# A state-space mixer's loop over batches, written out as straight code on every engine

## The chip, the cores and the metric

The kernel runs on one core of a Trainium2 chip (trn2). Its five engines (PE for matrix products, DVE for vector work, ACT for activations, POOL, and SP, which here only issues transfers) each run an instruction stream of their own and meet through semaphores. The metric is the device time of one execution in microseconds, the median over several.

## The reference

The input has 8 batches of 1024 tokens with 256 features. Three blocks follow each other: a feed-forward block on 4-bit quantised values, a selective-scan mixer, and the feed-forward block once more. The change touches only the mixer:

```python
x = x + 0.5 * ffn(layernorm(x))
x = x + mixer(layernorm(x))          # the part that the change touches
x = x + 0.5 * ffn(layernorm(x))

# mixer, per batch: 512 channels, 16 states each, 1024 steps in time
xz = norm(h) @ in_proj_w;  x, z = split(xz)
x = silu(causal_conv4(x))
delta = softplus((x @ x_proj_w)[:, :64] @ dt_proj_w + dt_proj_b)
h_t = exp(delta_t * A) * h_(t-1) + delta_t * B_t * x_t       # per channel and state
y_t = sum over states of h_t * C_t  +  D * x_t
out = (y * silu(z)) @ out_proj_w
```

The 512 x 16 sequences in time of a batch are worked on as 64 tiles of 128 partitions and 1024 steps, a tile being 8 channels with 16 states.

## The kernel before

`mixer` cuts its work into rounds, one for a batch. A round has 64 **slots**, and a slot does one of the 64 scan tiles: PE repeats the rows of delta times x onto the 128 partitions (`replicate`, L1226, into `mix_ps_du`), DVE multiplies them by B (L1102), ACT takes the exponential for the decay (L1037, into `mix_decay`, whose rows SP spreads by a transfer, L876, six slots ahead), DVE runs the scan (L1086, into `mix_scan`), POOL multiplies by C (L929), and PE sums over the states (`sum_quad`, L1208 and L1212, into `mix_ps_y`). So DVE has a product and a scan in every slot.

Between them lies the rest of the layer, spread over the slots by a table, `JOBS`: small matrix products of kinds T, P, C, X, B, D, Z and O (transpose, in-projection, convolution, x-projection, B and C, delta, gate, out-projection), most of them for the batch of the next round; O is for the batch before. For O, DVE adds the residual (L1116); at slot 4 of every 16 it gates the finished chunk (L1111); BN_STATS and BN_AGGR (L1127, L1135) belong to the norm of the next batch. Each engine has its own function `program(r, R, full)`, which emits one round: `r` decides at build time which parts exist and which half of each double buffer is used, and `R` is the round's number, from which every count that a semaphore is waited for is worked out, and every address in DRAM.

`rounds` calls `program` for r from -1 to 8, ten rounds. Round -1 only prepares batch 0, round 8 only finishes batch 7. Rounds -1, 0, 7 and 8 are straight code. Rounds 1 to 6 are a hardware loop on each engine (`Fori`): three iterations with two rounds in each, in which `R` is a register expression, `it * 2 + 1` or `it * 2 + 2`. So at the end of round 2 and of round 4 each engine branches back, and at the end of round 6 it falls through. There every count and address comes out of register instructions, such as

```python
n = R * 64 + (slot + 1)
dve.wait_ge(exp_done, n)
dve.wait_ge(dbu_done, n)
if slot >= 8 or r > 0:
    dve.wait_ge(y_made, R * 16 + (slot - 8) // 4 + 1)
```

at L1082 to L1085. The engines go around the loop on their own: there is no barrier at its end. The feed-forward blocks have loops of their own (`span`, L32).

## Time and profile before

| | |
|---|---|
| median of 3 runs | 3338.32 us (3337.11 to 3343.49) |
| the profiled execution, its own time | 3331.19 us |
| its span, first to last instruction | 3329.3 us |
| first scan of round 0 to last of round 7 | 750.17 to 2704.05 us |
| mean granted TensorE clock | 0.884 |

The views used below are: a table of stretches of time, with the busy time of each engine; the timeline of one engine, with the idle time in front of an instruction and what ended it in square brackets (nothing stands there where the idle time is under about 0.1 us); and the list of waits of one engine. "issue" as the reason means that nothing that the profile records (no semaphore, no transfer) ended the wait. Register and branch instructions have no rows of their own in these views; they show only as idle time of the engine. Round r begins here with the scan of its slot 0 on DVE.

### The profile page before, as it was taken

The numbers are of one execution on the slowest core, as the hardware profiler recorded it, in microseconds if no ns is written. First come the engines' busy times: TensorE is split into PE (matmuls) and PEld (weight loads), VectorE is DVE, ScalarE is ACT, GpSimd is POOL, SyncE is SP. The second block draws the span as 40 slices with busy tenths as digits, with TensorE's granted clock in tenths as the row PEclk, the third lists the DMA queues.
The fourth block names the chain that finished last, engine by engine and source line by source line (L and its number), as shares of the span: only waits on it lengthen the run. The fifth ranks groups of instructions, "written<-read, shape, count | busy, mean of one in ns | idle before, by whom it ended". The sixth has DMA issues, their size and how long they took to land. (4 is left out here: it accounts for less than half of the span.)

```text
span 3329.3 us, 33530 instructions
## 1 busy us (share of the span) xinstructions
PE 2725.0 (82%) x10221; PEld 1387.1 (42%) x10221; DVE 2664.6 (80%) x2530; ACT 1682.9 (51%) x2331; POOL 2171.1 (65%) x1219
## 2 busy tenths in 40 slices
PE   3999999767877878868878868878867658999999
PEld 1556556542424414414414414414312124656565
DVE  6777777309998998988998998998999956777774
ACT  3444444246664665764665764665664513444442
POOL 4555554218877877877877877877877734555552
PEclk9999999887978978978978978978977669999999
DMA  3011100018686775776776775775876820100100
GB/s 101 19 32 32 32 26 22 26 29 200 161 191 155 171 180 155 180 172 155 169 182 155 183 169 155 176 176 155 187 176 160 204 85 24 32 26 32 32 26 19
DMA packets 164631, 379.73 MB, mean 114 GB/s; under 512 B 21990, under 2 KB 81446, under 8 KB 164198
## 3 DMA queue, kind: packets, MB, share of 16 engines
q1 hardware_dynamic: 146678, 358.67, 44.0%
q10 hardware_dynamic: 17776, 18.94, 2.0%
q8 instruction: 81, 1.33, 0.2%
q14 instruction: 96, 0.79, 0.1%
HBM read 308.26 MB, written 44.11 MB: 106 GB/s over the span
## 5 line engine op out<-in xcount | busy, mean ns | idle before, releaser
L929 POOL TENSOR_TENSOR mix_scan<-mix_scan,mix_bc 128x1024 f32<-128x1024 f32 x512 | 1205.8, 2357 | 436.7 <-DVE mix_scan L1086 436.2
L1086 DVE TENSOR_TENSOR_SCAN mix_scan<-mix_decay,mix_ps_du 128x1024 f32<-128x1024 f32 x512 | 1169.5, 2284 | 70.3 <-ACT mix_decay L1037 27.0
L1226 PE MATMUL mix_ps_du<-mix_stack,mix_sel 96*128 96x512 bf16 x1024 | 371.2, 451 | 430.3 <-DVE mix_scan L1086 397.8
L1102 DVE TENSOR_TENSOR mix_ps_du<-mix_ps_du,mix_bc 128x1024 f32<-128x1024 f32 x512 | 618.3, 1208 | 97.8 <-PE mix_ps_du L1226 85.1
L649 PE MATMUL ffn_ps_gate_up<-ffn_w_gate_up,ffn_xT 128*128 128x512 f32 (+1 forms) x1536 | 662.4, 568 | 14.6 <-DVE ffn_h L456 13.0
L1037 ACT ACTIVATE mix_decay<-mix_decay,mix_a_neg 128x1024 f32<-128x1024 f32 x512 | 571.5, 1141 | 146.0 <-DMA mix_decay<-delta_rows 140.6
L679 PE MATMUL ffn_ps_down<-ffn_w_down,ffn_hT 128*128 128x256 f32 (+1 forms) x1536 | 388.5, 395 | 11.4 <-ACT ffn_hT L584 11.4
L1226 PEld LDWEIGHTS mix_ps_du<-mix_stack,mix_sel 96*128 96x128 bf16 x1024 | 77.1, 103 | 765.9 <-DVE mix_scan L1086 646.1
L649 PEld LDWEIGHTS ffn_ps_gate_up<-ffn_w_gate_up,ffn_xT 128*128 128x128 f32 x1536 | 273.5, 191 | 281.5 <-issue 231.2
L456 DVE TENSOR_TENSOR ffn_h<-ffn_silu_gate,ffn_ps_gate_up 128x704 f32<-128x704 f32 x128 | 113.6, 887 | 302.7 <-ACT ffn_silu_gate L589 302.7
L1208 PE MATMUL mix_ps_y<-mix_scan,mix_red 128*32 128x512 f32 x2048 | 344.6, 755 | 4.8 <-POOL mix_scan L929 4.8
L570 POOL TENSOR_TENSOR ffn_h_scaled<-ffn_h,ffn_h_recip 128x1408 f32<-128x1408 f32 x64 | 184.8, 2888 | 225.1 <-ACT ffn_h_recip L629 225.1
L679 PEld LDWEIGHTS ffn_ps_down<-ffn_w_down,ffn_hT 128*128 128x128 f32 (+1 forms) x1536 | 277.1, 192 | 107.7 <-issue 57.1
L1167 PE MATMUL mix_ps_job<-mix_xin,mix_conv_diag 128*128 128x256 f32 x1024 | 271.5, 414 | 19.9 <-ACT mix_xin L982 19.8
L583 ACT ACTIVATE ffn_hT<-ffn_ps_turned 128x640 f32<-128x640 f32 x128 | 90.1, 704 | 325.8 <-PE ffn_ps_turned L661 325.8
L1167 PEld LDWEIGHTS mix_ps_job<-mix_xin,mix_conv_diag 128*128 128x128 f32 x1024 | 206.6, 207 | 106.3 <-issue 46.9
L564 POOL TENSOR_TENSOR ffn_hq<-ffn_h_scaled,ffn_h_scale 128x1408 f32<-128x1408 f32 x64 | 165.8, 2590 | 78.1 <-DVE ffn_h_scaled L509 73.9
L550 POOL TENSOR_TENSOR ffn_mv<-ffn_mv,ffn_eps 128x2 f32<-128x2 f32 x64 | 33.1, 517 | 253.5 <-DVE ffn_mv L491 249.0
L988 ACT ACTIVATE mix_u<-mix_ps_job,mix_conv_b 128x256 f32<-128x256 f32 x128 | 60.6, 474 | 206.2 <-PE mix_ps_job L1167 205.6
L1188 PE MATMUL mix_ps_job<-mix_hnT,mix_w_in 128*128 128x512 f32 x256 | 147.4, 705 | 6.5 <-ACT mix_hnT L967 6.4
L1160 PE MATMUL mix_ps_job<-mix_hnT,mix_w_in 128*128 128x256 f32 x512 | 131.1, 402 | 4.2 <-ACT mix_hnT L967 3.5
L1194 PE MATMUL mix_ps_job<-mix_w_out,mix_u 128*128 128x256 f32 x512 | 131.9, 417 | 1.4 <-DVE mix_u L1111 1.4
(131 smaller groups left out, 3515.0 us busy)
## 6 DMA issues: line engine op xcount, KB each, us to landing
mix_decay<-delta_rows SPq DMA_DIRECT2D x512, 512.0 KB, 7.5
mix_stack<-mix_parts SPq DMA_DIRECT2D x384, 64.0 KB, 2.0
delta_rows<-mix_delta SPq DMA_DIRECT2D x32, 512.0 KB, 3.1
ffn_x<-_attn_hidden_states_dram SPq DMA_DIRECT2D x32, 256.0 KB, 2.9
after_ffn<-ffn_y SPq DMA_DIRECT2D x32, 256.0 KB, 3.0
mix_x_tokens<-after_ffn SPq DMA_DIRECT2D x32, 256.0 KB, 5.5
mix_x_residual<-after_ffn ACTq DMA_DIRECT2D x32, 256.0 KB, 5.6
after_mixer<-mix_x_residual ACTq DMA_DIRECT2D x32, 256.0 KB, 5.1
```

The lines of the kernel that those rows point to most:

```text
L564: G.tensor_tensor(blocks(hq[:, l2, :]), blocks(hn[:, l2, :]), spread(hs[:, (j - 1) % 4, :]), ALU.mult).then_inc(sig.hq_done, 1)
L570: G.tensor_tensor(blocks(hn[:, j % 2, :]), blocks(h[:, j % 2, :]), spread(hr[:, :]), ALU.mult).then_inc(sig.hn_done, 1)
L649: ins = M(psG[:, lo:hi], xT[:, j % 2, (t * KX + k) * P:(t * KX + k + 1) * P], wgu[:, k, lo:hi], start=(k == 0), stop=(k == KX - 1))
L679: ins = M(psD[:, t, 0:D], hT[0:c, t, k * P:(k + 1) * P], wd[0:c, k, :], start=(k == 0), stop=(k == KH - 1))
L929: G.tensor_tensor(wt, wt, bc[:, r % 2, 1, :], ALU.mult).then_inc(hc_done, 1)
L1037: A.activation(da[:, at % SPREADS, :], da[:, at % SPREADS, :], ACT.Exp, scale=const.aneg[:, qi:qi + 1]).then_inc(exp_done, 1)
L1086: V.tensor_tensor_scan(w[:, slot % RING, :], da[:, slot % SPREADS, :], ps_du[:, slot % 2, :], 0.0, ALU.mult, ALU.add).then_inc(scan_done, 1)
L1102: V.tensor_tensor(ps_du[:, slot % 2, :], ps_du[:, slot % 2, :], bc[:, r % 2, 0, :], ALU.mult)\
L1167: ins = M(job[:, 0:QT], const.conv_diag[:, c, t, :], xin[:, c, t:t + QT], start=(t == 0), stop=(t == TAPS - 1))
L1188: ins = M(job, const.w_in[:, k, DI + c * P:DI + (c + 1) * P], hnT[:, par, k, h * 512:(h + 1) * 512], start=(k == 0), stop=(k == KD - 1))
L1208: ins = M(y[32 * q:32 * q + 32, :], const.red[:, i, :, :].rearrange("p a b -> p (a b)"), w[:, (4 * m + q) % RING, h * 512:(h + 1) * 512], ...
L1226: ins = M(ps_du[:, slot % 2, h * 512:(h + 1) * 512], const.sel[0:SEL, i, :], stack[:, c % 2, q, h * 512:(h + 1) * 512], start=True, stop=True)
```

## The change

`rounds` calls `program(r, r, False)` for all ten rounds, so that no loop is left in the mixer. With a plain number for `R`, every count is a constant in the wait, and every DRAM address a constant in the transfer. `full` was true in the loop only; for r from 1 to 6 the conditions in which it stands (`full or r + 1 < B`, `full or r >= 1`, `core`) come out the same, and so does the list of jobs. What is computed, and in which order, stays as it was.

```diff
-            pairs = (B - 2) // 2
-            for r in range(-1, 1):
-                program(r, r, False)
-            if pairs > 0:
-                with eng.Fori(0, pairs) as it:
-                    for k in range(2):
-                        program(1 + k, it * 2 + (1 + k), True)
-            for r in range(1 + 2 * pairs, B + 1):
+            for r in range(-1, B + 1):
                 program(r, r, False)
```

Seven lines go, so a line number L of the mixer before is L - 7 after, from L811 on.

The order of DVE's instructions at the end of the loop's body, before the change; the last product and scan are those of slot 63 of an even round (the scan is named SCALAR_TENSOR_TENSOR in these lists):

```order
L1086 SCALAR_TENSOR_TENSOR mix_scan<-mix_decay,mix_ps_du 128x1024 [waits mix_y_made,mix_dbu_done,mix_exp_done]
L1095 REGISTER_ALU
L1102 TENSOR_TENSOR mix_ps_du<-mix_ps_du,mix_bc 128x1024 [waits mix_rep_du]
L1086 SCALAR_TENSOR_TENSOR mix_scan<-mix_decay,mix_ps_du 128x1024 [waits mix_y_made,mix_dbu_done,mix_exp_done]
L811 REGISTER_ALU
L811 COMPARE_AND_BRANCH
```

The branch leads back to the top of the body, the first instructions of an odd round on DVE (ISA stands for a fused register instruction):

```order
L811 ISA
L1097 ISA [waits mix_rep_du]
L1102 TENSOR_TENSOR mix_ps_du<-mix_ps_du,mix_bc 128x1024 [waits mix_taken_B]
L1085 ISA [waits mix_dbu_done,mix_exp_done]
L1086 SCALAR_TENSOR_TENSOR mix_scan<-mix_decay,mix_ps_du 128x1024 [waits mix_y_made]
L1095 REGISTER_ALU
```

After the change, the same place on DVE, from the product of slot 62 of round 2 to the scan of slot 0 of round 3:

```order
L1095 TENSOR_TENSOR mix_ps_du<-mix_ps_du,mix_bc 128x1024 [waits mix_rep_du]
L1079 SCALAR_TENSOR_TENSOR mix_scan<-mix_decay,mix_ps_du 128x1024 [waits mix_y_made,mix_dbu_done,mix_exp_done]
L1095 TENSOR_TENSOR mix_ps_du<-mix_ps_du,mix_bc 128x1024 [waits mix_rep_du]
L1079 SCALAR_TENSOR_TENSOR mix_scan<-mix_decay,mix_ps_du 128x1024 [waits mix_y_made,mix_dbu_done,mix_exp_done]
L1095 TENSOR_TENSOR mix_ps_du<-mix_ps_du,mix_bc 128x1024 [waits mix_taken_B,mix_rep_du]
L1079 SCALAR_TENSOR_TENSOR mix_scan<-mix_decay,mix_ps_du 128x1024 [waits mix_y_made,mix_dbu_done,mix_exp_done]
```

The counter, the branch and the five register instructions are gone, and the product of slot 0 carries both of its waits itself.

Within a round on DVE, before the change: from behind the scan of slot 59 to the product of slot 61, in an even round. In front of the scan of slot 60, the first of a group of four, for which the count of `y_made` goes up by one, stands a register instruction which carries two of its three waits:

```order
L1095 REGISTER_ALU
L1102 TENSOR_TENSOR mix_ps_du<-mix_ps_du,mix_bc 128x1024 [waits mix_rep_du]
L1085 REGISTER_ALU [waits mix_dbu_done,mix_exp_done]
L1086 SCALAR_TENSOR_TENSOR mix_scan<-mix_decay,mix_ps_du 128x1024 [waits mix_y_made]
L1095 REGISTER_ALU
L1102 TENSOR_TENSOR mix_ps_du<-mix_ps_du,mix_bc 128x1024 [waits mix_rep_du]
```

After the change these slots read as the rows of the seam shown above do: product, scan, product, scan, with nothing between them, and the scan has its three waits again.

On PE the end of the loop's body, before (slots 62 and 63 of an even round), and under it the top of the body:

```order
L1226 MATMUL mix_ps_du<-mix_stack,mix_sel 128x512 [waits mix_scan_done]
L1226 MATMUL mix_ps_du<-mix_stack,mix_sel 128x512
L1208 MATMUL mix_ps_y<-mix_scan,mix_red 32x512 [waits mix_hc_done]
L1208 MATMUL mix_ps_y<-mix_scan,mix_red 32x512 x7
L811 REGISTER_ALU
L811 COMPARE_AND_BRANCH
```

```order
L811 ISA
L1224 ISA [waits mix_stacked_du0]
L1226 MATMUL mix_ps_du<-mix_stack,mix_sel 128x512 [waits mix_scan_done]
L1226 MATMUL mix_ps_du<-mix_stack,mix_sel 128x512
L1226 MATMUL mix_ps_du<-mix_stack,mix_sel 128x512 [waits mix_scan_done]
L1226 MATMUL mix_ps_du<-mix_stack,mix_sel 128x512
L1248 ISA
```

After the change, PE's same place between rounds 2 and 3:

```order
L1219 MATMUL mix_ps_du<-mix_stack,mix_sel 128x512 [waits mix_scan_done]
L1219 MATMUL mix_ps_du<-mix_stack,mix_sel 128x512
L1201 MATMUL mix_ps_y<-mix_scan,mix_red 32x512 [waits mix_hc_done]
L1201 MATMUL mix_ps_y<-mix_scan,mix_red 32x512 x7
L1219 MATMUL mix_ps_du<-mix_stack,mix_sel 128x512 [waits mix_scan_done,mix_stacked_du0]
L1219 MATMUL mix_ps_du<-mix_stack,mix_sel 128x512
L1219 MATMUL mix_ps_du<-mix_stack,mix_sel 128x512 [waits mix_scan_done]
```

Here too the matrix products stand in the same order, and the first two `replicate` of the next round follow the last sum directly.

## Rows read from the trace of the kernel before

**Rows 1.** The page, its costliest groups (line, counts, busy us, mean ns, idle before)

```profile
L1086 DVE TENSOR_TENSOR_SCAN mix_scan<-mix_decay,mix_ps_du 128x1024 f32<-128x1024 f32 x512 | 1169.5, 2284 | 70.3 <-ACT mix_decay L1037 27.0
...
L1102 DVE TENSOR_TENSOR mix_ps_du<-mix_ps_du,mix_bc 128x1024 f32<-128x1024 f32 x512 | 618.3, 1208 | 97.8 <-PE mix_ps_du L1226 85.1
```

**Rows 2.** Stretches of time, one for each of rounds 0 to 7

```profile
core 0: us, PE busy (x) PEld busy (x) DVE busy (x) ACT busy (x) POOL busy (x), PEclk, DMA share, GB/s
750.17:984.17 234.00, 177.36 (x676) 73.89 (x675) 224.25 (x148) 152.44 (x180) 189.69 (x100) 0.83 0.77 181
984.17:1231.58 247.41, 196.78 (x760) 89.68 (x759) 227.81 (x152) 151.07 (x179) 191.00 (x101) 0.85 0.71 171
1231.58:1483.22 251.64, 196.98 (x764) 89.01 (x763) 227.89 (x152) 152.22 (x181) 192.22 (x101) 0.85 0.72 173
1483.22:1729.86 246.64, 191.85 (x758) 87.36 (x758) 227.60 (x153) 150.14 (x178) 189.88 (x100) 0.86 0.69 165
1729.86:1980.95 251.09, 196.46 (x763) 89.05 (x763) 227.93 (x152) 151.68 (x180) 192.13 (x101) 0.85 0.72 174
1980.95:2228.32 247.37, 195.73 (x759) 89.33 (x758) 227.82 (x153) 150.91 (x179) 189.88 (x100) 0.84 0.68 165
2228.32:2473.03 244.71, 193.64 (x761) 87.95 (x761) 227.76 (x152) 151.28 (x179) 190.94 (x101) 0.86 0.71 171
2473.03:2704.05 231.02, 155.24 (x504) 41.61 (x502) 221.23 (x135) 108.22 (x107) 174.05 (x76) 0.68 0.67 162
```

**Rows 3.** Timeline of DVE, end of round 2 (start, us, instruction, idle before)

```profile
1472.82 2.29 DVE L1086 TENSOR_TENSOR_SCAN mix_scan<-mix_decay,mix_ps_du 128x1024 f32<-128x1024 f32 x1
1481.79 1.23 DVE L1102 TENSOR_TENSOR mix_ps_du<-mix_ps_du,mix_bc 128x1024 f32<-128x1024 f32 x1 [6.68 <-issue]
1483.22 2.29 DVE L1086 TENSOR_TENSOR_SCAN mix_scan<-mix_decay,mix_ps_du 128x1024 f32<-128x1024 f32 x1 [0.20 <-DVE mix_ps_du L1102]
```

**Rows 4.** Timeline of PE and of POOL, the same place

```profile
1478.22 1.89 PE L1226 MATMUL mix_ps_du<-mix_stack,mix_sel 96*128 96x512 bf16 x4 [5.47 <-issue]
...
1485.59 2.36 POOL L929 TENSOR_TENSOR mix_scan<-mix_scan,mix_bc 128x1024 f32<-128x1024 f32 x1 [8.06 <-DVE mix_scan L1086]
```

**Rows 5.** Timeline of DVE, end of round 4

```profile
1971.16 2.29 DVE L1086 TENSOR_TENSOR_SCAN mix_scan<-mix_decay,mix_ps_du 128x1024 f32<-128x1024 f32 x1
1979.52 1.23 DVE L1102 TENSOR_TENSOR mix_ps_du<-mix_ps_du,mix_bc 128x1024 f32<-128x1024 f32 x1 [6.07 <-issue]
```

**Rows 6.** Timeline of DVE, end of round 6, where the loop is left

```profile
2469.53 2.29 DVE L1086 TENSOR_TENSOR_SCAN mix_scan<-mix_decay,mix_ps_du 128x1024 f32<-128x1024 f32 x1
2471.74 1.21 DVE L1102 TENSOR_TENSOR mix_ps_du<-mix_ps_du,mix_bc 128x1024 f32<-128x1024 f32 x1
```

**Rows 7.** Timeline of DVE, slots 27 to 29 of round 1

```profile
1097.68 2.29 DVE L1086 TENSOR_TENSOR_SCAN mix_scan<-mix_decay,mix_ps_du 128x1024 f32<-128x1024 f32 x1
...
1101.29 2.29 DVE L1086 TENSOR_TENSOR_SCAN mix_scan<-mix_decay,mix_ps_du 128x1024 f32<-128x1024 f32 x1 [0.19 <-DVE mix_ps_du L1102]
...
1104.79 2.29 DVE L1086 TENSOR_TENSOR_SCAN mix_scan<-mix_decay,mix_ps_du 128x1024 f32<-128x1024 f32 x1
```

**Rows 8.** Waits of DVE in rounds 1 to 6 (total us, times, longest)

```profile
DVE mix_ps_du L1102 <- issue: 12.8, 2, 6.7
DVE mix_scan L1086 <- DVE mix_ps_du L1102: 12.4, 59, 0.6
```

**Rows 9.** Waits of DVE, straight code: round 0, then round 7

```profile
DVE mix_scan L1086 <- DVE mix_ps_du L1102: 0.2, 1, 0.2
...
DVE mix_scan L1086 <- issue: 0.9, 2, 0.4
```

**Rows 10.** Timeline of PE at slot 17, in round 1 and in round 2

```profile
1056.67 3.42 PE L1167 MATMUL mix_ps_job<-mix_xin,mix_conv_diag 128*128 128x256 f32 x8
...
1303.79 2.00 PE L1167 MATMUL mix_ps_job<-mix_xin,mix_conv_diag 128*128 128x256 f32 x8
```

**Rows 11.** Stretches of time around these two, with the granted clock

```profile
1054.00:1063.00 9.00, 8.13 (x27) 4.26 (x28) 8.84 (x8) 3.56 (x5) 7.21 (x8) 0.81 0.74 170
1300.00:1309.00 9.00, 7.37 (x31) 3.49 (x30) 8.91 (x7) 4.53 (x7) 6.72 (x8) 1.00 0.76 191
```

**Rows 12.** DMA queues in rounds 1 to 6 (packets, MB, share)

```profile
q8 instruction: 44, 0.72, 0.2%
q14 instruction: 61, 0.50, 0.1%
```

## The prediction

> **What bounds the kernel now.** I first read the groups of the page, for DVE's two instructions of a slot: a product of 1208 ns and a scan of 2284 ns [rows 1], together 3.49 us. Two scans that follow without an idle mark start 3.50 us apart, 1104.79 - 1101.29 [rows 7]. So in a plain slot DVE works without a gap and sets the pace; 64 such slots are 224 us. Next I cut the time into rounds. In every one DVE is busy for 221 to 228 us out of 231 to 252, while PE reaches at most 197, POOL 192 and ACT 152 [rows 2]. The whole mixer is thus DVE's chain, and what the change is worth is read from the idle time of DVE, and from nothing else.
>
> The same table has an experiment in it: rounds 0 and 7 are straight code already, rounds 1 to 6 are the loop. Rounds 2 and 4, which end in a taken branch, last 251.64 and 251.09 us; round 6, the same code but left at its end, 244.71 [rows 2]. The odd rounds 1, 3 and 5 last 247.41, 246.64 and 247.37. Round 0 has no O jobs and round 7 nothing of a next batch, so their 234.00 and 231.02 are not to be set against the loop's as a whole; single waits can be.
>
> **Term 1: the two branches back.** What the reader is to see at the end of round 2: the scan of slot 63 starts at 1472.82, the product after it only at 1481.79, with 6.68 us idle that no semaphore and no transfer ended, and the next scan at 1483.22 [rows 3]. PE stood idle too, 5.47 us, also for "issue", and POOL 8.06 us [rows 4]. Each engine comes to its own branch at its own time; PE, which runs ahead, has its gap first, and DVE's own gap is what the chain has to bear. From scan to scan it is 1483.22 - 1472.82 = 10.40 us. Where the same code goes on without a branch back, the product follows the scan after 2471.74 - 2469.53 = 2.21 us [rows 6], and the next scan 3.50 us after the first, as in round 6 (2473.03 is where its stretch ends [rows 2]). The seam thus costs 10.40 - 3.50 = 6.90 us, of which 0.10 is the register work of term 2; I count 6.80. At the end of round 4 it is 1980.95 - 1971.16 = 9.79 us [rows 2, 5], so 9.79 - 3.61 = 6.18. Together **13.0 us**.
>
> Is that pause given back in the round behind it, because the other engines catch up? Round 3 and round 5 follow a pause, round 1 follows straight code: 246.64 and 247.37 against 247.41 [rows 2]. So 0.8 and 0.0 us are given back, and 12.2 is the lower bound of this term, 13.0 the upper. I take 13.0: rounds 5 and 1 agree to 0.04, and the 0.8 has another likely cause, below.
>
> What the Trainium skill has on it: "Runtime: NRT & Kernel Launch", section "Instruction fetch mechanics", says that fetching ahead is sequential only and that a taken branch to a target which isn't held any more makes the engine wait for its code. The 6.68 us of "issue" are what this looks like here.
>
> **Term 2: register instructions.** The loop works its counts out in registers. Most of it is done under a running scan or product and costs nothing: plain slots of the loop last 3.50 us too [rows 7]. But where the count for `y_made` goes up, once in four slots, the register instruction in front of the scan (slot 28 in the rows) also carries the wait for the product, so it can't run before that has ended: 0.19 us idle, and 1101.29 - 1097.68 = 3.61 us in place of 3.50. The loop's six rounds have 59 such waits, 12.4 us in total [rows 8]; round 0, straight, has one [rows 9]. The regular ones are some nine to ten a round and cost 0.10 to 0.11 each beyond a plain slot. The few that are longer, up to 0.6, are ended by something else too. With 54 x 0.10 I take **5.4 us**; the upper bound is 59 x 0.11 = 6.5, the lower one 0, if the second wait, now in an instruction of its own, takes the same time. I take the value near the upper end, since round 0 has exactly that form and just one mark.
>
> **What costs nothing.** The register work of PE, ACT, POOL and SP, and SP's addresses: these engines have 50 to 100 us of slack in a round [rows 2]. If that cover were gone, it would show as DVE waiting for PE or ACT, as it does around the O jobs in the first 16 slots, and a shorter PE or ACT would help there; I count no gain. The number of matrix products, activations and transfers is unchanged. Entry into the loop costs one more 0.1. What was late at the seam was the code alone; the next thing DVE would wait for there is PE's `replicate`, which in straight code comes 2 slots ahead and is ready.
>
> **The sum.** 13.0 + 5.4 = 18.4 us. The profiled execution's own 3331.19 becomes 3312.8, its span of 3329.3 becomes 3310.9. The median of the runs shown lies 7.1 above the profiled one, 3338.32; with the same difference the median after is **3319.9 us**, 0.55% less.
>
> **The term that can't be placed: TensorE's clock.** The odd rounds are longer than the even ones without their seams: the odd mean is 247.14; the even are 251.64 - 6.80 = 244.84, 251.09 - 6.18 = 244.91 and 244.71, mean 244.82. The 2.3 us come from PE. Eight matrix products of the convolution jobs of slot 17 take 3.42 us in round 1 and 2.00 in round 2 [rows 10], because the granted clock was 0.81 of full speed in that stretch, part of it at 1.2 GHz, against 1.00, all at 2.4 GHz [rows 11]; ACT then waits for PE, and DVE for ACT. Nothing in the code differs there. It depends on how the clock's falls meet the slots, and that repeats because an iteration of the loop always lasts the same. Without the seams every round is shifted against them. If all six rounds look like the even ones, 3 x 2.3 = 7 us more are gained; if all look like the odd ones, 7 are lost. I take the middle, no change, and give the range the 7 on both sides: gains of 11.4 to 25.4, or 3313 to 3327. About 3 us of spread between runs (3337.11 to 3343.49) widens it to 3310 to 3330.
>
> **The rivals.**
> 1. *Only the branches are worth something* (the second wait costs as much as the register instruction did): gain 13.0, 3325. Against it stands round 0 with its single mark [rows 9].
> 2. *The gap at the seam is not the branch's*, but a wait at the round's change that straight code has as well; then 5.4 alone is gained, 3333, within 0.2%. For it: no view names what ended the gap. Against it: at the end of round 6, the same position in the same code, the product follows after 2.21 us [rows 6]. The skill's "Advanced Engine Details and Errata", section "Control Flow Timing", gives a compare-and-branch about 108 ns; by it two seams would be worth 0.2 us and the time would come to this rival's. The trace doesn't agree: 6.68 and 6.07 us idle.
> 3. *Slower: straight code is read too late.* Each engine must be supplied with new code all the way. In rounds 1 to 6 that was 0.72 + 0.50 MB at 0.3% of the queues [rows 12]. If supply failed somewhere in a round as it does at a seam, at some 6.5 us each, three failures would use up the 18.4; one in each of six rounds costs 39, and the time is 3338 - 18 + 39 = 3359. Against it: rounds 0 and 7 are straight, and DVE's waits for "issue" in round 7 are 0.9 us in all [rows 9]. Within the loop's 500 us body there is no such wait either: both that exist are at the seams [rows 8].
>
> **How the numbers follow.** The forecast, both terms with the clock's share anywhere between its ends: 0.75. Rival 1: 0.12, which lies in the range. Rival 2, or another way to end within 0.2% (6.7 us, about what a measurement of this kernel can tell from no change): 0.06. Rival 3: 0.03. The rest, 0.04, is a gain beyond 28 us, if PE's and ACT's register work does count in the first 16 slots. Faster is 0.75 + 0.12 + 0.04 = 0.91, the same 0.06, slower 0.03. The range of 3310 to 3330 leaves out rivals 2 and 3, the large gain, and what of the clock falls outside: under 0.2.
>
> **What the changed profile would show.** Term 1: no idle time of 6 us for "issue" on DVE between rounds 2 and 3, and 4 and 5; scans 3.50 us apart there. Term 2: DVE's waits "mix_scan from mix_ps_du" fall from 59 to a handful, with 3.50 from the scan of slot 27 to that of slot 28. The clock: rounds 1 to 6 each between 243.9 and 246.3 us, and where they differ, conv matrix products of PE of 3.4 us instead of 2.0. The prediction is wrong if DVE waits for "issue" in the middle of rounds, if the seams stay, or if rounds 1 to 6 come to lie outside 242 to 248.

## The result, and the profile after

The kernel after takes **3310.31 us** (median of 6 runs, 3307.86 to 3317.17), the kernel before 3339.18 us in the same measurement (6 runs, 3336.17 to 3345.31). The ratio is 0.992, with an interval of 0.9905 to 0.9935: faster by 0.8%. The profiled execution of after took 3310.79 us, against 3331.19 of the one before. The forecast was 3319.9 us for the median, in 3310 to 3330, and 3312.8 us for the profiled execution.

The stretches of time, one for each round, in the kernel after, with the columns of [rows 2]:

```profile
748.71:982.17 233.46, 173.44 (x675) 71.98 (x675) 224.13 (x148) 152.40 (x180) 189.61 (x100) 0.84 0.77 182
982.17:1227.56 245.39, 196.63 (x762) 89.89 (x761) 227.81 (x153) 150.89 (x179) 190.95 (x101) 0.85 0.72 171
1227.56:1469.77 242.21, 191.77 (x762) 87.05 (x761) 227.70 (x152) 151.09 (x179) 190.95 (x101) 0.87 0.72 174
1469.77:1717.58 247.81, 195.90 (x761) 87.92 (x760) 228.08 (x153) 151.35 (x179) 190.95 (x101) 0.85 0.71 170
1717.58:1962.90 245.32, 195.23 (x761) 88.49 (x762) 227.97 (x152) 151.19 (x179) 191.00 (x101) 0.85 0.72 172
1962.90:2207.84 244.94, 194.12 (x762) 88.23 (x761) 227.61 (x153) 150.99 (x179) 190.99 (x101) 0.85 0.72 172
2207.84:2453.06 245.22, 196.61 (x762) 89.71 (x761) 227.77 (x152) 150.87 (x179) 190.96 (x101) 0.85 0.72 172
2453.06:2684.22 231.16, 157.32 (x504) 41.68 (x502) 221.46 (x135) 108.26 (x107) 174.12 (x76) 0.67 0.67 161
```

DVE is busy in every round as long as before; what fell is its idle time. Rounds 2 and 4, which lasted 251.64 and 251.09 us before, are now 242.21 and 245.32. From the first scan of round 0 to the last of round 7 it is 1935.5 us, against 2704.05 - 750.17 = 1953.9 before: 18.4 us less. The remaining 2.0 us of the profiled difference lie outside the mixer, 1.5 ahead of it and 0.5 behind.

The timeline of DVE at the end of round 2, which answers to [rows 3]:

```profile
1466.27 2.29 DVE L1079 TENSOR_TENSOR_SCAN mix_scan<-mix_decay,mix_ps_du 128x1024 f32<-128x1024 f32 x1
1468.47 1.21 DVE L1095 TENSOR_TENSOR mix_ps_du<-mix_ps_du,mix_bc 128x1024 f32<-128x1024 f32 x1
1469.77 2.29 DVE L1079 TENSOR_TENSOR_SCAN mix_scan<-mix_decay,mix_ps_du 128x1024 f32<-128x1024 f32 x1
```

The seam is gone: the product follows the scan after 2.20 us in place of 8.97, and the next scan after 3.50 in place of 10.40. All seven changes of round are 3.50 us. All waits of DVE in rounds 1 to 6 (total us, times, longest), as in [rows 8]:

```profile
DVE mix_x_residual L1109 <- PE mix_ps_job L1187: 41.2, 18, 3.7
DVE mix_scan L1079 <- ACT mix_decay L1030: 21.2, 14, 2.1
DVE mix_ps_du L1095 <- PE mix_ps_du L1219: 11.4, 15, 1.7
DVE mix_u L1104 <- PE mix_ps_y L1205: 4.1, 6, 0.8
```

Both lines of [rows 8] are missing, the 12.8 us for "issue" and the 59 short waits between product and scan. DVE waits only for PE and ACT now. The same four lines of before come to 41.6, 22.1, 6.7 and 6.5 us, 76.9 in all against 77.9: nothing of the gain comes from the other engines, and almost nothing was given back. The instruction queues moved less, not more, than before over the whole execution (1.33 and 0.79 MB then):

```profile
q8 instruction: 75, 1.23, 0.2%
q14 instruction: 66, 0.54, 0.1%
```

### The profile page after: what moved, and what is told of

It reads as the page before. It is cut to its first block and busy times, and to the rows that moved or that the text cites. A ratio compares the mean times of both kernels' runs of the same rounds, so it can differ in the third digit from the quotient of the medians.

```text
span 3309.0 us, 31136 instructions
## 1 busy us (share of the span) xinstructions
PE 2718.9 (82%) x10221; PEld 1382.5 (42%) x10221; DVE 2664.7 (81%) x2530; ACT 1681.7 (51%) x2331; POOL 2170.9 (66%) x1219
## 3 DMA queue, kind: packets, MB, share of 16 engines
q8 instruction: 75, 1.23, 0.2%
## 5 line engine op out<-in xcount | busy, mean ns | idle before, releaser
L1095 DVE TENSOR_TENSOR mix_ps_du<-mix_ps_du,mix_bc 128x1024 f32<-128x1024 f32 x512 | 618.1, 1207 | 89.5 <-PE mix_ps_du L1219 89.4
L589 ACT ACTIVATE ffn_silu_gate<-ffn_ps_gate_up 128x704 f32<-128x704 f32 x128 | 96.9, 757 | 71.5 <-PE ffn_ps_gate_up L649 71.5
```

Source lines behind the costliest of these rows:

```text
L1095: V.tensor_tensor(ps_du[:, slot % 2, :], ps_du[:, slot % 2, :], bc[:, r % 2, 0, :], ALU.mult)\
```

## The experiments

Every kernel was timed beside the kernel before on the same chip. The kernel before ran 72 times as the partner of a comparison, with a mean of 3335.2 us (3324.2 to 3345.9), the kernel after 12 times, with 3311.5 (3305.1 to 3317.2). "Loop" below means the kernel before, "straight" the one after. The seams and the pace of a slot are read from the starts of the scans in each kernel's timeline of DVE. One more view is used: asked for a single line of the kernel, the profile also shows the register, branch and wait instructions of that line, under the name DVEq for DVE, with how many there are, their shortest, median and longest duration in ns, and the start of the first and of the last in us.

| kernel | us, median | ratio to before, interval | seams after rounds 2 and 4, us | short waits product to scan, rounds 1 to 6 |
|---|---|---|---|---|
| one seam | 3323.89 | 0.9967 (0.9954 to 0.998) | 9.67, 3.50 | 39 |
| only DVE straight | 3320.15 | 0.9957 (0.9943 to 0.9971) | 7.97, 7.71 | none |
| only DVE in the loop | 3337.45 | 1.0005 (0.9994 to 1.0016) | 10.08, 9.76 | 59 |
| `y_made` ahead of the product | 3359.30 | 1.0077 (1.0064 to 1.009) | 17.41, 17.44 | none |
| `y_made` first, loop | 3354.59 | 1.0048 (1.0031 to 1.0064) | 9.86, 9.45 | 3 |
| padded | 3345.83 | 1.003 (1.0017 to 1.0043) | 15.69, 16.38 | 57 |
| before again | 3333.12 | 0.9992 (0.9978 to 1.0006) | 10.13, 10.82 | 58 |
| after again | 3312.59 | 0.9921 (0.9901 to 0.994) | 3.50, 3.50 | none |
| `y_made` first, straight | 3319.13 | 0.996 (0.9946 to 0.9973) | 3.54, 3.54 | none |
| `dbu_done` first, straight | 3308.73 | 0.993 (0.9914 to 0.9946) | 3.45, 3.45 | 5 |
| all loops straight | 3307.04 | 0.9927 (0.9913 to 0.9942) | 3.50, 3.50 | none |
| the last two together | 3298.99 | 0.9892 (0.9873 to 0.991) | 3.45, 3.44 | 5 |

### One seam instead of two

```diff
-            pairs = (B - 2) // 2
+            pairs = (B - 4) // 2
```

The loop covers rounds 1 to 4 only, so that each engine branches back once, after round 2; rounds 5 and 6 are straight.

> The loop covers rounds 1 to 4 in two iterations, rounds 5 and 6 are straight code; one taken branch is left instead of two. Two-term theory: one gap of 6.1 to 6.7 us on DVE after round 2, none after round 4, register marks in four rounds only, time 6.5 + 1.8 = 8.3 us below before. Rival (the loop also sets how the clock's falls meet the slots, and what the change gained beyond 18.4 us comes from breaking that pattern): more than 12 us are gained.

Measured: 3323.9 us (median and mean), 9.8 under the mean of before in the same comparison (3333.7). The timeline of DVE at the end of round 2, and at the end of round 4, where the loop is now left:

```profile
1483.73 1.23 DVE L1102 TENSOR_TENSOR mix_ps_du<-mix_ps_du,mix_bc 128x1024 f32<-128x1024 f32 x1 [5.96 <-PE mix_ps_du L1226]
...
1973.20 2.29 DVE L1086 TENSOR_TENSOR_SCAN mix_scan<-mix_decay,mix_ps_du 128x1024 f32<-128x1024 f32 x1
...
1976.70 2.29 DVE L1086 TENSOR_TENSOR_SCAN mix_scan<-mix_decay,mix_ps_du 128x1024 f32<-128x1024 f32 x1
```

The seam follows the branch: where none is taken, it is 3.50 us. The short waits fell from 59 to 39, as rounds 5 and 6 lost theirs. One seam (6.2) and some 20 short waits (2.0) are 8.2 us of the 9.8. The length of the one profiled execution doesn't show them: its mixer took 1955.9 us, 2.0 more than that of before, while slot 51, of which more below, took 7.6 us in rounds 2 and 6 and 4.45 in both in before. So the terms are read from their rows, and the gain from many executions.

The first row is also a lesson in reading: the same stall is here put down to PE's `replicate`, because PE's own code came late in the same microseconds. PE's products start at 1480.87. In the kernel with only DVE straight, below, DVE's product follows PE's start after 1.07 us (1477.04 - 1475.97), here only after 2.86: by then it was no longer PE that it waited for.

The branch itself can be seen in the kernel before. These are DVE's branch and the first instruction of the body at the end of round 2, then the branch at the end of round 6, which is not taken, and the instruction behind it:

```profile
L811 DVEq COMPARE_BRANCH  x1: 72/72/72, 1472.9 to 1472.9; - x1
L811 DVEq FUSED_REGOPS  x1: 85/85/85, 1481.6 to 1481.6; - x1
```

```profile
L811 DVEq COMPARE_BRANCH  x1: 55/55/55, 2469.6 to 2469.6; - x1
...
L1097 DVEq EVENT_SEMAPHORE  x1: 21/21/21, 2469.7 to 2469.7; - x1
```

The branch takes 72 ns, and then nothing runs on DVE's stream of instructions for 8.6 us. The first thing that runs is a register instruction that waits for no semaphore. Some 2.1 us of this lie under the scan that was started before the branch. In the 13 branches back of DVE that the traces hold, the pause is between 7.7 and 9.0 us. Where the branch is not taken, the next instruction follows at once.

### Whose branch is it: DVE alone, and all but DVE

```diff
-        def rounds(eng, program):
+        def rounds(eng, program, straight=False):
-            pairs = (B - 2) // 2
+            pairs = 0 if straight else (B - 2) // 2
```

One kernel calls it with `True` for DVE only, the other for SP, POOL, ACT and PE, but not for DVE.

> Only DVE's stream is straight code, the other four engines keep the loop. If the gap at the seam is each engine's own, DVE's 6.7 us for issue go, but PE's gap of 5.5 us and ACT's of 8 us stay and DVE waits for PE or ACT there, by 3 to 5 us per seam, since PE runs only one slot ahead. Gain 5.4 + 2 x (1.5 to 3.5) = 8 to 12 us. Rival (DVE's branch alone makes the seam): all of the 18.4 us are gained.

> DVE alone keeps the loop, PE, ACT, POOL and SP are straight code. If the seam is DVE's own code that comes late, the 6.7 and 6.1 us for issue on DVE and the 59 marks stay, and the time is within 3 us of before. Rival (the register work of the other engines, or their gaps, is what the change removed): a gain of 10 us or more.

With DVE alone straight the time is 3320.2 us; the mean of its six runs, 3321.0, lies 12.7 under before, just above the 8 to 12 expected and clearly under the rival's 18.4. (Its profiled execution was the longest of the six, 3326.9 us; its mixer took 1952.9, only 1.0 less than in before, with 12.16 us for slot 51 of round 5.) With DVE alone in the loop it is 3337.5 us, the same as before. The end of round 2 in the first of the two, on DVE and on PE:

```profile
1470.39 2.29 DVE L1086 TENSOR_TENSOR_SCAN mix_scan<-mix_decay,mix_ps_du 128x1024 f32<-128x1024 f32 x1
1477.04 1.23 DVE L1102 TENSOR_TENSOR mix_ps_du<-mix_ps_du,mix_bc 128x1024 f32<-128x1024 f32 x1 [4.36 <-PE mix_ps_du L1226]
```

```profile
1475.97 1.89 PE L1226 MATMUL mix_ps_du<-mix_stack,mix_sel 96*128 96x512 bf16 x4 [5.81 <-issue]
```

and DVE in the second:

```profile
1475.22 2.29 DVE L1086 TENSOR_TENSOR_SCAN mix_scan<-mix_decay,mix_ps_du 128x1024 f32<-128x1024 f32 x1
1483.87 1.23 DVE L1102 TENSOR_TENSOR mix_ps_du<-mix_ps_du,mix_bc 128x1024 f32<-128x1024 f32 x1 [6.36 <-issue]
```

DVE's own branch alone makes the whole seam (10.08 us scan to scan). The branches of the other four leave 7.97 - 3.50 = 4.5 us of it, and the wait is for PE: PE has its code wait of 5.81 us ahead of the products that DVE needs next, and its lead is less than that. The two lie side by side and must not be added; only when both are gone is the seam 3.50. No wait for POOL or ACT stands in DVE's rows there: the scan starts 1.32 us after its product, as in a plain slot. The short waits go with DVE's form alone: none in the first, 59 in the second.

### A wait moved ahead of the product

```diff
-                if slot >= 8 or r > 0:
-                    dve.wait_ge(y_made, R * 16 + (slot - 8) // 4 + 1)
                 V.tensor_tensor_scan(
...
+                        if slot % 4 == 0 and (slot >= 8 or r > 0):
+                            dve.wait_ge(y_made, R * 16 + (slot - 8) // 4 + 1)
                         dve.wait_ge(rep_du, n)
```

The loop stays. The scan has two waits, and nothing that needs a register stands between product and scan.

> The loop stays as it was before; on DVE the wait for y_made, whose count goes up once in four slots, is put in front of the slot's product instead of the scan, where its register instruction runs under the scan before. Theory (two terms: seams 13.0 us, register wait 5.4 us): the seams stay at 10.4 and 9.8 us from scan to scan, the waits of mix_scan for mix_ps_du fall from 59 to a few, slot 27 to 28 takes 3.50 instead of 3.61, and the time falls by 5.4 us (0.16%) against before. Rival (the 0.1 us is the second wait, not the register instruction): the marks stay or move to the product and the time doesn't change. Rival (y_made is late): slots get longer by up to 1 us and the time rises.

The short waits went, as expected, and the kernel got slower all the same, by 3358.9 - 3333.7 = 25.2 us between the means. DVE at the end of round 2, and two of its waits in rounds 1 to 6:

```profile
1474.34 2.29 DVE L1084 TENSOR_TENSOR_SCAN mix_scan<-mix_decay,mix_ps_du 128x1024 f32<-128x1024 f32 x1
1490.42 1.23 DVE L1102 TENSOR_TENSOR mix_ps_du<-mix_ps_du,mix_bc 128x1024 f32<-128x1024 f32 x1 [13.79 <-issue]
1491.76 2.29 DVE L1084 TENSOR_TENSOR_SCAN mix_scan<-mix_decay,mix_ps_du 128x1024 f32<-128x1024 f32 x1
```

```profile
DVE mix_ps_du L1102 <- issue: 27.6, 2, 13.8
DVE mix_ps_du L1102 <- PE mix_ps_y L1212: 19.2, 14, 4.1
```

Two things were not foreseen. The stall at each seam is twice as long, 13.8 us; the two seams are 17.41 + 17.44 - 10.40 - 9.79 = 14.7 us longer than in before. The timeline shows it as one wait, but the rows of single lines show two. DVE branches at 1474.8, the body's first instruction runs at 1483.8, two more register instructions follow, and the last of these, the third of the body, runs at 1484.1. The product starts at 1490.42:

```profile
L1097 DVEq FUSED_REGOPS  x1: 46/46/46, 1484.1 to 1484.1; - x1
```

That is 9.0 us, three instructions, and 6.3 us more. And second, the product now waits for `sum_quad`, which it does not need; part of these 19.2 us replaces other waits for PE. A plain slot lasts 3.52 us in this form. As a test of term 2 the kernel was useless, since it changed more than the term. It raised the question why one seam can have a stall of 6.7 us and another one of 13.8.

### Where the branch's target lies: padded

```diff
             V = nc.vector
+            for i in range(14):
+                V.memset(padding[:, i:i + 1], 0.0)
```

Fourteen tiny instructions on DVE ahead of round -1, on a scratch tile of their own. The loop's body does not change, but it lies 14 instructions further on.

> The kernel before with 14 tiny memsets of a scratch tile of its own on DVE ahead of the mixer's round -1, where DVE is idle; they only move the loop's code by 14 instructions, as early_y did with the 14 instructions it has more ahead of the loop. Theory (code comes in pieces of fixed size, and a branch to the end of a piece must wait for two of them): DVE's gap at each seam rises from 6.7 to 13.8 us, the time by 2 x 7 = 14 us (0.4%) against before. Rival (early_y's doubled gap came from its waits for y_made): gaps of 6.7 us and the same time as before.

Measured: 3345.8 us, with a mean 10.0 over that of before in the same comparison (3335.6). DVE at the end of round 2:

```profile
1468.43 2.29 DVE L1089 TENSOR_TENSOR_SCAN mix_scan<-mix_decay,mix_ps_du 128x1024 f32<-128x1024 f32 x1
1477.66 1.23 DVE L1105 TENSOR_TENSOR mix_ps_du<-mix_ps_du,mix_bc 128x1024 f32<-128x1024 f32 x1 [6.95 <-issue]
1484.12 2.29 DVE L1089 TENSOR_TENSOR_SCAN mix_scan<-mix_decay,mix_ps_du 128x1024 f32<-128x1024 f32 x1 [5.22 <-ACT mix_decay L1038]
```

One stall of 13.8 us and 14 us more of time were expected. There are two stalls, one in front of the product and one of 5.22 us in front of the scan behind it, which the profile puts down to ACT. The seams are 15.69 and 16.38 us, 11.1 more than in the repeat of before (10.13 and 10.82), and the time rose by 10.0. ACT is not what the scan waited for, as the two instructions between product and scan show, the first with the wait for the product and the second with the wait for ACT:

```profile
L1086 DVEq EVENT_SEMAPHORE  x1: 21/21/21, 1484.0 to 1484.0; - x1
...
L1088 DVEq FUSED_REGOPS  x1: 46/46/46, 1484.0 to 1484.0; - x1
```

Neither waited: they took 21 and 46 ns, as in a seam of before, but they came only 6.3 us after the product had started. So again nothing runs for 8.5 us behind the branch (1468.9 to 1477.4), then three instructions do, the product being the third, and then nothing for 6.3 us. It is the very place of the second pause in the kernel with the moved wait, whose body also lies 14 instructions further on than in before (1209 instead of 1195 of DVE's instructions ahead of it in the traces). The third instruction is a register instruction there and the product here, so it is the place in the code that counts, not what stands there. The scratch tile and the 14 instructions, in a stretch where DVE is idle, are all else that was added. So the price of a branch back depends on where its target lies. The Trainium skill, "Runtime: NRT & Kernel Launch", section "Instruction fetch mechanics", says that the instruction memory of most engines holds two blocks of 16 KiB and is refilled a block at a time. The first queue's packets are of that size here, 1.23 MB / 75 = 16.4 KB. By that rule a target shortly ahead of a block's end needs the next block almost at once, and the second pause behind the third instruction, in both kernels, is what a block's end there would look like. No other shift was tried, so that the blocks are of this size is not shown here.

### The order of the three waits

```diff
                 n = R * 64 + (slot + 1)
-                dve.wait_ge(exp_done, n)
-                dve.wait_ge(dbu_done, n)
                 if slot >= 8 or r > 0:
                     dve.wait_ge(y_made, R * 16 + (slot - 8) // 4 + 1)
+                dve.wait_ge(exp_done, n)
+                dve.wait_ge(dbu_done, n)
```

This edit was made to the loop and to the straight kernel. It leaves all waits where they are and changes only the order in which they are written.

> The loop as before; in front of DVE's scan the three waits are written in another order, y_made first, so that the register instruction that works out its count carries no wait and can run under the product. Nothing else changes, nor does the length of the code ahead of the loop on DVE. Theory (term 2 is the register instruction behind the product): the 59 marks fall to a few, the seams stay at about 10 us from scan to scan, and the time falls by 5.4 us (0.16%). Rival (the 0.1 us is the third wait as such): 59 marks and the same time. Early_y, which moved the wait in front of the product, lost 23 us; if that came from the wait for y_made ahead of the product and from the doubled seam, none of it shows here.

> Straight code with the order of waits of y_first. In y_first the marks were gone and yet every plain slot took 3.543 us instead of 3.500, so loop and straight code differ there by the two seams alone. Two-term theory: 13 to 14 us below y_first's 3353, so 3339 us, with slots of 3.543. Rival (the loop costs something else besides seams and marks, as the 24 to 29 us between before and after suggest): 3333 us or less.

A third kernel, straight, has the order `dbu_done`, `exp_done`, `y_made`:

> Straight code in which the scan's waits are written with dbu_done first, then exp_done, then y_made. In the traces the scan itself carries the wait written first, and an instruction of its own in front of it the other two; plain slots took 3.500 us with exp_done on the scan and 3.543 with y_made on it. Theory (with the product's signal awaited by the scan itself, the instruction in front is done before the product ends and leaves the path): slots of 3.45 us or less, over 400 plain slots 20 us less than the changed kernel's 3311. Rival (what counts is the propagation of the product's signal, the same for both): 3.50 and the same time. Rival (the scan is issued later if it waits itself, as with y_made): slots of 3.54 and 18 us more.

The timeline of DVE in a plain slot: first `y_made` first, in the loop, then the kernel after, then `dbu_done` first:

```profile
1105.67 1.21 DVE L1102 TENSOR_TENSOR mix_ps_du<-mix_ps_du,mix_bc 128x1024 f32<-128x1024 f32 x1
1107.01 2.29 DVE L1086 TENSOR_TENSOR_SCAN mix_scan<-mix_decay,mix_ps_du 128x1024 f32<-128x1024 f32 x1
```

```profile
1464.97 1.21 DVE L1095 TENSOR_TENSOR mix_ps_du<-mix_ps_du,mix_bc 128x1024 f32<-128x1024 f32 x1
```

```profile
1102.78 1.21 DVE L1095 TENSOR_TENSOR mix_ps_du<-mix_ps_du,mix_bc 128x1024 f32<-128x1024 f32 x1
1104.02 2.29 DVE L1079 TENSOR_TENSOR_SCAN mix_scan<-mix_decay,mix_ps_du 128x1024 f32<-128x1024 f32 x1
```

From the product's start to the scan's it is 1.34, 1.30 (1466.27 - 1464.97) and 1.24 us; the way from the scan to the next product is 2.20 in all three. So a plain slot lasts 3.54, 3.50 or 3.45 us, on the order of lines alone. Shortest is the order in which `dbu_done`, the semaphore that the product itself raises, is written first. In the traces the wait written first is the one that the scan carries itself, and the other two stand in an instruction ahead of it. This instruction in the kernel after, twice, and with `y_made` first, straight:

```profile
L1078 DVEq EVENT_SEMAPHORE  x2: 2484/2932/3381, 1467.2 to 1469.8; - x2
```

```profile
L1078 DVEq EVENT_SEMAPHORE  x1: 50/50/50, 1101.5 to 1101.5; - x1
```

In the kernel after it holds `y_made` and `dbu_done`, stands waiting while the product runs, and the scan follows it. With `y_made` first it holds the waits for the product and for ACT, and runs for 50 ns between the product's end and the scan. With `dbu_done` first it is over before the product ends, and the scan starts 0.03 us after the product's end (1102.78 + 1.21). In the slots of 3.61 us of the loop [rows 7] three instructions follow one another behind the product: one of 21 ns with the wait for `dbu_done`, the register instruction of 40 ns with that for `exp_done`, and the scan with `y_made`. So what lengthens the slot is what still has to run between the product's end and the scan. Other orders were not tried.

The times do not follow the slots alone, and all three forecasts of a time failed. With `y_made` first the loop was to gain 5.4 us and lost 17.6 (3353.1 against 3335.6, means); the short waits went, but every plain slot got 0.04 us longer. The same order in straight code was to take 3339 us and takes 3319.7, so its rival held. `dbu_done` first was to gain 20 us over the kernel after and gained 2.8 (3308.7 against 3311.5), which isn't clear of the spread between runs; in the profiled executions its mixer is 8.9 us shorter (1926.6 against 1935.5). With `y_made` first the loop and the straight kernel are 33 apart, where seams and short waits explain 12. In the two profiled executions, which lie 37 apart, DVE's waits for PE and ACT in rounds 1 to 6 account for 20 more: 89.5 us in the loop (44.6 + 23.8 + 12.5 + 8.6), 69.3 in the straight kernel (43.7 + 20.4 + 3.7 + 1.5). Stretches of 10 us before the gate of slot 51 in round 2, in the loop and in the straight kernel:

```profile
1422.80:1432.80 10.00, 10.00 (x23) 2.54 (x22) 9.60 (x6) 6.27 (x9) 6.63 (x3) 0.66 1.05 240
```

```profile
1423.00:1433.00 10.00, 9.44 (x35) 2.58 (x34) 9.60 (x6) 7.82 (x11) 6.80 (x3) 1.00 1.03 247
```

TensorE had a granted clock of 0.66 in the one, so part of it at 1.2 GHz, and 1.00, all at 2.4 GHz, in the other. PE, busy throughout, counts 23 matrix products there instead of 35, and slot 51 took 7.61 us (1430.77 to 1438.38) instead of 4.45. The same slot took 7.6 to 7.9 us in rounds 4, 5 and 6 of the loop too, and 4.45 in all of them in the straight kernel: four times 3.2 us.

### Repeats, and what is left to gain

> The kernel before, unchanged, to see how much two executions differ and where. Seams of 10 us from scan to scan and 54 to 59 register marks in any execution; the rounds without their seams vary by up to 3 us each where TensorE's granted clock falls at other slots. Rival (the first profiled execution, 3331 us, had short seams by luck): here the seams are longer.

> The changed kernel, unchanged, as a second sample. The two-term theory gives 18.4 us less than before for the mean of many executions; the first comparison showed 29 us between the medians and 20 between the profiled executions. If 18.4 is right, the medians differ here by 15 to 22 us. Rival (the loop costs more than the two terms, by slots that fall badly on the clock's falls in each iteration): 24 us or more again.

The kernel before against itself gives 0.9992 (0.9978 to 1.0006), the kernel after once more 0.9921 (0.9901 to 0.994). The medians differ by 3334.2 - 3312.6 = 21.7 us, within the 15 to 22 expected, but the means by 24.0, which was the rival's mark, so this comparison doesn't decide between the two. The profiled executions differ by 3338.70 - 3316.99 = 21.7 us, after 20.4 in the first pair. Their mixers took 1962.9 and 1945.3 us, 9 to 10 more than the same code in the first pair.

In the next kernel the feed-forward blocks' `Fori` of `span` is written out as well:

```diff
-    rounds = (last - body - lo) // body
-    for i in range(first, lo):
-        step(i, base + i)
-    with eng.Fori(0, rounds) as it:
-        for j in range(body):
-            step(lo + j, it * body + (base + lo + j))
-    for i in range(lo + rounds * body, last):
+    for i in range(first, last):
         step(i, base + i)
```

> The changed kernel with the loops of both feed-forward blocks written out too. Their bodies are short (on DVE 254 instructions, on ACT 196), and the taken branches in them show no gap in the trace. Theory (only a branch back over more code than an engine holds has to wait): the same time as the changed kernel within 2 us. Rival (each taken branch and register count costs): 5 us or more less.

It takes 3307.0 us; the mean of 3308.1 is 3.4 under that of all runs of after, between the theory's 2 and the rival's 5, and just about the spread of single runs. In the profile the blocks are shorter, 744.5 us ahead of the first scan (after 748.7 and 747.4) and 619.2 behind the last (624.8 and 622.5): 3.6 and 4.4 us on average. The kernel with both edits, below, has 744.0 and 620.9, while the twelve profiled executions with these loops have 746.1 to 750.7 and 621.8 to 627.1. So the gain in the blocks looks real. It isn't the branches back: there is one on DVE in each block, and in the first the body's first instruction runs less than 0.4 us behind it (342.4 to 342.8), not 8 us. What makes it was not tested. The last kernel has both edits, `dbu_done` first and no loop at all:

> The straight kernel with two more edits at once: the order of the scan's three waits is dbu_done, exp_done, y_made, and the two feed-forward blocks' loops are written out as well. Each was run alone: the order gave 3308.7 us, the loops 3308.1, the straight kernel itself 3311.5 as the mean of its twelve timed runs. Theory A, the two act in different stretches and add up: 3311.5 - 2.8 - 3.4 = 3305 us; in the profile a plain slot lasts 3.446 us, and first to last scan of the mixer lies near 1927 to 1936 us, the feed-forward blocks near 744.5 ahead of it and 619 behind. Theory B, they don't add up (one of them was a chance of the runs): 3308 to 3312. Theory C, by slots alone: some 350 plain slots at 0.054 us less would give 19 us, 3311.5 - 19 - 3.4 = 3289; it would need the gated slots and the clock's falls to be no worse than in the straight kernel, which the run with the order alone did not show.

3299.0 us, ratio 0.9892 (0.9873 to 0.991) to before, and 12.7 under after by the means (3298.8 and 3311.5). Theory A expected 3305, 6.2 under the mean of after: the two edits together gave more than their single runs, and less than the slots alone would (theory C, 3289). With six runs between 3289.1 and 3308.9 it isn't clear that it is more than the sum. The mixer took 1929.6 us. DVE's waits for PE and ACT:

```profile
DVE mix_x_residual L1103 <- PE mix_ps_job L1181: 43.5, 18, 3.7
DVE mix_scan L1073 <- issue: 21.9, 12, 2.2
DVE mix_ps_du L1089 <- PE mix_ps_du L1213: 13.7, 18, 2.1
DVE mix_u L1098 <- PE mix_ps_y L1199: 7.3, 10, 0.9
DVE mix_scan L1073 <- ACT mix_decay L1024: 3.1, 4, 1.4
```

The "issue" here is no late code. With `exp_done` waited for in an instruction of its own, which the view does not show, the waits for ACT of the kernel after (21.2 us, 14 times) appear under this name. In all, the five lines are 89.5 us against 77.9 in after: some 12 us of what the shorter slots gain are given back as waits for PE and ACT, in these two executions. How much of it comes from a DVE that gets there earlier, and how much from the clock, was not separated.

## Why the prediction was right, point by point

- **Direction and bound: right.** DVE's chain set the end; its busy time is unchanged and the whole profiled gain in the mixer is idle time of DVE.
- **Term 1, the branches, 13.0 us: right.** Both seams went to 3.50 us. Removing one removed one (one seam), and DVE's own branch is enough to make the whole of it (only DVE in the loop). The text named DVE's own gap as what the chain bears; it did not say that PE's gap alone would still have cost 4.5 us, and that PE had to be straight too for the full term. It took PE's `replicate` to come 2 slots ahead; in time it is one: in the kernel after PE starts it at 1468.61 for the product at 1471.97, since it waits for the scan two slots before. In the repeat of before the seams cost 13.7 by the same sum, (10.13 - 3.61) + (10.82 - 3.61). That none of the pause is given back behind it fits the sum of DVE's other waits, 76.9 and 77.9 us, to within what the clock moves.
- **Term 2, the register instruction with the waits, 5.4 us: right in the profile.** The 59 waits are gone, slot 27 to slot 28 lasts 3.50 in rounds 1 to 6, and only DVE's form decides it.
- **The sum: 18.4 us forecast, 18.4 in the mixer**, 20.4 in the profiled executions, for which 3312.8 was forecast and 3310.8 measured. That the mixer agrees to a tenth is luck. Two executions of each kernel were profiled, with mixers of 1953.9 and 1962.9 us before and 1935.5 and 1945.3 after; paired the other ways they give 8.6 or 27.4. What is shown without luck are the terms' own rows.
- **From the profiled execution to the median: the step that was off.** The text added the 7.1 us by which the runs shown lay above the profiled execution, "with the same difference" after. This difference belonged to one execution, not to the kernel: 3331.19 was 4.0 under the mean of all 72 runs of before, while 3310.79 of after is 0.7 under its own. Measured over all runs the gain is 3335.2 - 3311.5 = 23.7 us. 18.4 to 19.1 are the two terms; some 5 us are left. They go along with the clock: the mean granted clock of the runs of before is 0.882 (66 of the 72 have one on record), that of after 0.886, and at the same clock the two are closer. At 0.884 before has ten runs with a mean of 3332.1 us and after three with 3316.1, 16.0 apart. Whether straight code raises the clock, or something else moves both, was not tested. Hence 3310.3 at the very edge of the range of 3310 to 3330.
- **The clock, 7 us either way: the mechanism right, the bounds for single rounds too narrow.** Rounds 1 to 6 were to lie between 243.9 and 246.3 us each; four do, and rounds 2 and 3 lie at 242.21 and 247.81. In the repeat of after, round 3 took 250.9. Their sum was forecast at 1488.9 - 18.4 = 1470.5 us, and is 1470.9. In round 3 the gate of slot 51 shows it. DVE's timeline there, and the stretches of 10 us around this slot and around that of round 2:

```profile
1668.40 2.29 DVE L1079 TENSOR_TENSOR_SCAN mix_scan<-mix_decay,mix_ps_du 128x1024 f32<-128x1024 f32 x1
1672.39 1.23 DVE L1095 TENSOR_TENSOR mix_ps_du<-mix_ps_du,mix_bc 128x1024 f32<-128x1024 f32 x1 [1.70 <-PE mix_ps_du L1219]
1674.45 1.23 DVE L1104 TENSOR_TENSOR mix_u<-mix_ps_y,mix_silu_z 128x1024 f32<-128x1024 f32 x1 [0.82 <-PE mix_ps_y L1205]
1675.59 2.28 DVE L1079 TENSOR_TENSOR_SCAN mix_scan<-mix_decay,mix_ps_du 128x1024 f32<-128x1024 f32 x1
```

```profile
1664.00:1674.00 10.00, 10.00 (x31) 2.30 (x30) 6.72 (x4) 6.31 (x9) 4.71 (x2) 0.76 0.62 143
1418.60:1428.60 10.00, 7.35 (x30) 1.80 (x28) 9.82 (x7) 8.31 (x10) 6.86 (x3) 1.00 0.83 200
```

  Slot 51 took 1675.59 - 1668.40 = 7.19 us in round 3, where PE's clock was 0.76, and 4.45 in round 2, at 1.00. The forecast looked for the clock in the convolution jobs of slot 17 alone; it falls elsewhere as well, and slot 51 is the dearest place here (4.9 us over its shortest in rounds 1 to 6), with slot 22 close behind. The text also thought that the pattern repeats because an iteration of the loop always lasts the same. It repeats without a loop, and from execution to execution: in the two of after, rounds 4 to 6 last 245.32, 244.94 and 245.22 us, and 245.34, 244.94 and 245.23, and slot 51 takes 7.19 us in round 3 and 6.56 in round 4 in both.
- **Rival 1** (only the branches): out. The 59 waits are gone, and two kernels that differ mainly in them and the seams, only DVE straight and before, are 12.7 us apart with seams that explain only 10.40 - 7.97 + 9.79 - 7.71 = 4.5; 8.2 are left, of which term 2 is 5.4.
- **Rival 2** (the gap isn't the branch's): out, by the kernel with one seam, and by the branch's own row, behind which nothing runs for 8.6 us.
- **Rival 3** (straight code read too late): out. DVE has no wait for "issue" in rounds 1 to 6 of after, and with all loops written out the instruction queues still move only 1.36 and 0.59 MB.

## What to carry to other kernels

Here a hardware loop over a long body cost the engine that sets the pace some 7 us for each branch back, and up to twice that depending on where the target lies. With a trip count of three it is worth writing the loop out, on all engines that feed the critical one. Look for "issue" in front of the body's first instruction, and then at the rows of the loop's own line, which show the branch and what runs next; a stall that the timeline puts down to another engine can be the same thing. On an engine that works without a gap, the instructions between two dependent operations count singly. Writing the wait for the semaphore that comes last first, so that the waiting instruction carries it itself, made the slot 0.05 us shorter; read that from start to start, and don't count on it in the time, of which it gave 2.8 us where 20 were expected. A median can't be forecast from one profiled execution to better than the spread between executions, here about 5 us either way, so take the difference of the medians from several runs and the terms from the profile.

## What the runs showed of the hardware

- **The price of a branch back moves with the code's place**: DVE's stream of instructions paused 8.6 us behind the branch in before, 9.0 + 6.3 with a wait moved ahead of the product, and 8.5 + 6.3 when 14 instructions were put ahead of the loop, the second pause behind the third instruction of the body both times. A timing difference between two variants of a loop kernel can be this alone.
- **Several waits on one instruction are not one wait.** Their written order alone decides whether a slot lasts 3.45, 3.50 or 3.54 us; of what that would be over the mixer, the times of the straight kernels show 11.0 us between the slowest order and the fastest (3319.7 - 3308.7), since waits for PE and ACT take part of it back.
- **The clock's falls are worth about as much as a term of this change.** The same mixer code took 1935.5 and 1945.3 us in two executions; the same slot takes 4.45 us or 7.2 to 7.9, by whether TensorE is granted 2.4 GHz there throughout or 1.2 GHz for a part. With `y_made` first, the loop waited 20 us longer for PE and ACT than the straight kernel with the same slots.
